# Experts of a small language-model tower: up products with the weights stationary, and the shared FFN by chunk

## What is computed

```python
h = take(W.T, x)                                   # 2048 rows of 128
h = h + mixer(layernorm(h))                        # tanh recurrence, gate, output product
xf = layernorm(h)                                  # [2048, 128]
idx, wts = top_1(xf @ gate_w.T)                    # one of 8 experts; softmax over one is 1
h1 = silu(xf @ w1[e].T) * (xf @ w3[e].T)           # inner width 512
y  = h1 @ w2[e].T                                  # back to 128
y += gelu(xf @ sw1.T) @ sw2.T                      # shared FFN, inner width 512
out = h + y
```

## Time and profile before

| | us |
|---|---|
| median of 3 runs | 190.79 (190.6 to 192.27) |
| the profiled execution | 191.11 |
| its span, first to last instruction | 189.3 |
| PE busy | 140.8 (74%) |
| DVE busy | 127.2 (67%) |
| ACT busy | 103.9 (55%) |
| POOL busy | 83.0 (44%) |

### The profile page before, as it was taken

How to read it: one execution, slowest core, us unless ns; L and a number is a source line. 1 busy time by engine, 2 the same in 40 slices (tenths; PEclk the granted TensorE clock), 3 DMA queues, 4 the chain that set the end, 5 groups by cost and what they waited for, 6 DMA issues and landing times.

```text
span 189.3 us, 3242 instructions
## 1 busy us (share of the span) xinstructions
PE 140.8 (74%) x1001; PEld 103.1 (54%) x1001; DVE 127.2 (67%) x364; ACT 103.9 (55%) x241; POOL 83.0 (44%) x77
## 2 busy tenths in 40 slices
PE   0106987697888888886894699990899999999710
PEld 0105865465666567763442699660476666776510
DVE  0245767838699857996681999651577888887720
ACT  2002343799569973787899970342256565666300
POOL 3767855500000001422000364373678888866580
PEclk9999999999999999999999579999589999999985
DMA  5663346994000000111100022321123243433331
GB/s 141 171 169 124 109 142 213 323 402 198 0 0 0 3 3 0 57 57 55 59 0 0 0 88 81 139 59 42 16 43 44 43 42 35 39 31 33 28 31 14
DMA packets 9955, 14.37 MB, mean 76 GB/s; under 512 B 1936, under 2 KB 4624, under 8 KB 9936
## 3 DMA queue, kind: packets, MB, share of 16 engines
q1 hardware_dynamic: 5904, 10.45, 16.1%
q0 software_dynamic: 4032, 3.67, 12.6%
HBM read 10.71 MB, written 3.41 MB: 75 GB/s over the span
## 4 chain that ended last, share of the span: by engine, by line
PE 40%; ACT 18%; DVE 11%; POOL 10%; issue 7%; DMA 7%; another core or an unknown queue 3%; SPq 1%; POOLq 0%
PE bank L647 13%; PE bank L592 7%; PE bank L674 7%; POOL emb_rows L364 6%; ACT attn_out L719 5%; PE bank L660 4%; ACT states L696 3%; DMA w_sb<-w 3%; DMA emb_rows<-emb,tok_sb 3%; PE bank L474 3%; ACT w_hl L729 3%; ACT states L755 2%; ACT w_hl L731 2%; POOL rstd L396 1%
## 5 line engine op out<-in xcount | busy, mean ns | idle before, releaser
L415 POOL DMA_INDIRECT out<-w_sb,row_of x20 | 31.4, 1570 | 13.7 <-DVE w_sb L1179 10.6
L474 PE MATMUL bank<-states,sq_sb 128*128 128x128 f32 x112 | 27.7, 331 | 6.4 <-ACT states L696 1.3
L647 PE MATMUL bank<-w_hl,xblk_t 128*128 x120 | 30.4, 392 | 0.6 <-issue 0.6
L474 PEld LDWEIGHTS bank<-states,sq_sb 128*128 128x128 f32 x112 | 17.8, 200 | 15.0 <-ACT states L696 14.2
L396 POOL TENSOR_TENSOR rstd<-vareps,cst 128x2 f32<-128x2 f32 x8 | 5.6, 697 | 46.6 <-DVE vareps L836 46.6
L472 PE MATMUL bank<-x_in,sq_sb 128*128 128x128 f32 x112 | 23.7, 295 | 2.2 <-ACT x_in L689 2.2
L797 ACT ACTIVATE w_sb<-bank,factor 128x512 f32<-128x512 f32 x20 | 13.8, 688 | 20.1 <-PE bank L647 14.6
L696 ACT ACTIVATE states<-bank 128x128 f32<-128x128 f32 x56 | 15.5, 276 | 14.9 <-PE bank L474 12.6
L674 PE MATMUL bank<-w_hl,w_sb 128*128 x160 | 17.5, 255 | 7.3 <-DVE w_sb L1179 7.3
L472 PEld LDWEIGHTS bank<-x_in,sq_sb 128*128 128x128 f32 x112 | 18.2, 203 | 3.4 <-ACT x_in L689 2.3
L408 POOL DMA_INDIRECT w_sb<-x_rows,row_in x16 | 15.4, 963 | 9.0 <-issue 6.9
(11 more groups left out here) (157 smaller groups left out, 284.2 us busy)
## 6 DMA issues: line engine op xcount, KB each, us to landing
w_sb<-w SPq DMA_DIRECT2D x24, 256.0 KB, 6.6
x_rows<-norm SPq DMA_DIRECT2D x4, 256.0 KB, 2.4
out<-attn_out SPq DMA_DIRECT2D x4, 256.0 KB
late<-places SPq DMA_DIRECT2D x1, 619.5 KB, 8.1
sw_sb<-sw SPq DMA_DIRECT2D x2, 256.0 KB
cst<-consts SPq DMA_DIRECT2D x1, 420.0 KB
sq_sb<-sq SPq DMA_DIRECT2D x1, 384.0 KB
out<-w_sb,row_of POOLq DMA_INDIRECT x20
```

The costliest lines, as they stand in the source:

```text
L415: pool.indirect_dma_start(out=out, out_offset=bass.IndirectOffsetOnAxis(ap=row_of[:, k:k + 1], axis=0), in_=out_blk[k % RING], in_offset=N ...
L474: pe.matmul(pre, at, states[:, i * COLS:(i + 1) * COLS], start=False, stop=True).then_inc(pre_ready, 1)
L647: mm = pe.matmul(hb[:], xblk_t[:, k % 3, b * P:(b + 1) * P], w[:, bass.ds(e * INNER + a * EXPERTS * INNER, INNER)], start=(j == 0), stop=( ...
```

## The change

- **Expert up products**: the weights become the stationary operand (128 columns of the inner width at a time), the transposed block the moving one. 24 matmuls of 128 columns in place of 6 of 512. The result has the inner width on its rows, so the transposes of the product and `turned` go; ACT and DVE take high and low half from `prod` in SBUF.
- **Two banks for the down product** (`ys`), and its wait for the output reaches back one block more.
- **Shared FFN by chunk**: `down_part(n)` runs the 12 matmuls of chunk n for four tiles as soon as `act_low` n is there; a product of zeros opens each group's bank. ACT takes high halves between the gelus, 8 behind (GELU_LEAD); gelu 0 comes inside the loop of pairs; the silu table is loaded behind the first `take_turned`. The inverse of the routing stands behind up product 13 (INVERT_AT = 14).
- **Gathers**: 16 ahead (AHEAD), each waiting for the landing of the one two before (IN_FLIGHT), a drain ahead of block 12.
- **Normalisation** of the last two pairs (LAST_NORMS) on DVE; **halves**: w1's upper high halves on ACT, all low halves of w2 before the attention end; SPREAD_STEPS 36 to 34, HIGH_STEP 38 to 36.

```diff
-SPREAD_STEPS = (22, 36)
-HIGH_STEP = 38
+SPREAD_STEPS = (22, 34)
+HIGH_STEP = 36
+GELU_LEAD = 8
+INVERT_AT = 14
+LAST_NORMS = 2
-AHEAD = 13
+AHEAD = 16
+IN_FLIGHT = 2
-DRAIN_AT = 6
-TURNED_FIRST = (1, 2, 2, 3, 4, 4, 5)
+DRAIN_AT = 12
-        rows_t, turned = (bank[3], bank[6]), (bank[4], bank[7])
+        rows_t, ys = (bank[3], bank[6]), (bank[6], bank[7])
...
             for k in range(AHEAD):
-                if 2 <= k < 5:
-                    pool.wait_ge(act_low, 4 * k)
-                elif k == 5:
-                    pool.wait_ge(base_ready, 3)
-                elif k >= 6:
-                    pool.wait_ge(blk_turned, TURNED_FIRST[k - 6])
                 if k == DRAIN_AT:
+                    pool.wait_ge(xblk_in[k - 1], 16)
                     pool.drain()
+                elif k >= IN_FLIGHT:
+                    pool.wait_ge(xblk_in[k - IN_FLIGHT], 16)
                 take_block(k)
...
+            def down_part(n):
+                g, i = divmod(n, IC)
+                if i == 0 and g >= 2:
+                    pe.wait_ge(base_ready, g - 1)
+                if i == 0:
+                    pe.matmul(bank[2 + g % 2][:], zeros[:], zeros[:, 0:1].to_broadcast([P, GC]), start=True, stop=False)
+                pe.wait_ge(act_low, n + 1)
+                for t in range(4):
                     for j, (a, b) in enumerate(halves):
                         mm = pe.matmul(bank[2 + g % 2][:, t * P:(t + 1) * P],
                                        (act_hi, act_lo)[a][:, g, i, t * P:(t + 1) * P],
                                        sw2_hl[:, b, i * P:(i + 1) * P],
-                                       start=(i == 0 and j == 0), stop=(i == IC - 1 and j == 2))
+                                       start=False, stop=(i == IC - 1 and t == 3 and j == 2))
...
-            for n in range(6, GROUPS * IC):
+            for n in range(6, INVERT_AT):
                 up(n)
+            pe.wait_ge(hots_ready, 1)
+            for t in range(TILES):
+                mm = pe.matmul(bank[4][:, 0:BLOCKS], lane_hot[:, :, t], nth_row[:, :, t],
+                               start=(t == 0), stop=(t == TILES - 1))
+            mm.then_inc(inverse_done, 1)
+            for n in range(INVERT_AT, GROUPS * IC):
+                up(n)
...
-            for m in range(TILES):
-                down(m)
-                if m == TILES - 4:
+            for n in range(GROUPS * IC):
+                down_part(n)
+                if n == GROUPS * IC - 3:
                     turn_block(0)
-                if m == TILES - 2:
-                    turn_block(1)
+            turn_block(1)
-            pe.wait_ge(w_split, 2)
+            pe.wait_ge(w_split, 3)
...
                     for w_hl, hb in ((w1_hl, bank[u]), (w3_hl, bank[2 + u])):
                         w = w_hl[:].rearrange("d h c -> d (h c)")
-                        for j, (a, b) in enumerate(halves):
-                            mm = pe.matmul(hb[:], xblk_t[:, k % 3, b * P:(b + 1) * P],
-                                           w[:, bass.ds(e * INNER + a * EXPERTS * INNER, INNER)],
-                                           start=(j == 0), stop=(j == 2))
+                        for i in range(IC):
+                            for j, (a, b) in enumerate(halves):
+                                mm = pe.matmul(hb[:, i * P:(i + 1) * P],
+                                               w[:, bass.ds(e * INNER + (a * EXPERTS * INNER + i * P), P)],
+                                               xblk_t[:, k % 3, b * P:(b + 1) * P],
+                                               start=(j == 0), stop=(j == 2))
                         mm.then_inc(h_done, 1)
...
-                if live(1):
-                    pe.wait_ge(prod_ready, k)
-                    if static is None or static >= 3:
-                        pe.wait_ge(prod_low, k - 2)
-                    for i in range(IC):
-                        mm = pe.transpose(turned[1 - u][:, i * P:(i + 1) * P], prod[:, 1 - u, i * P:(i + 1) * P], ident)
-                    mm.then_inc(prod_turned, 1)
                 if live(2):
                     pe.wait_ge(prod_low, k - 1)
-                    if static is None or static >= 3:
-                        pe.wait_ge(outb_ready, k - 2)
+                    if static is None or static >= 4:
+                        pe.wait_ge(outb_ready, k - 3)
...
-                            mm = pe.matmul(bank[6][:, 0:width], (prod_hi, prod_lo)[a][:, u, i * P:(i + 1) * P],
+                            mm = pe.matmul(ys[u][:, 0:width], (prod_hi, prod_lo)[a][:, u, i * P:(i + 1) * P],
...
-            act.wait_ge(w_split, 1)
-            for n in range(GROUPS * IC):
-                gelu(n)
-            act.activation(table_probe[:], half_bg[0:1, 0:1], ACT.Silu)
-            for n in range(GROUPS * IC):
-                act_high_half(n)
+            for n in range(1, GROUPS * IC + GELU_LEAD):
+                if n < GROUPS * IC:
+                    gelu(n)
+                if n >= GELU_LEAD:
+                    act_high_half(n - GELU_LEAD)
...
-                    act.wait_ge(prod_turned, k)
+                    act.wait_ge(prod_ready, k)
-                    act.activation(prod_hi[:, 1 - u, :], turned[1 - u][:], ACT.Copy).then_inc(prod_high, 1)
+                    act.activation(prod_hi[:, 1 - u, :], prod[:, 1 - u, :], ACT.Copy).then_inc(prod_high, 1)
...
             take_turned(0)
+            act.activation(table_probe[:], half_bg[0:1, 0:1], ACT.Silu)
             take_turned(1)
...
-            w1_low(slice(4 * INNER, 8 * INNER)).then_inc(w_split, 1)
+            dve.wait_ge(w1_high, EXPERTS // 2)
+            w1_low(slice(3 * INNER, 8 * INNER)).then_inc(w_split, 1)
...
+            def norm_last(n):
+                dve.wait_ge(rstd2_ready, n + 1)
+                for t in range(2 * n, 2 * n + 2):
+                    dve.tensor_scalar(norm2[:, t, :], attn_out[:, t, :], meanvar2[:, t, 0:1], rstd2[:, t:t + 1],
+                                      ALU.subtract, ALU.mult).then_inc(last_norm, 1)
...
-                    dve.tensor_tensor(prod_lo[:, 1 - u, :], turned[1 - u][:], prod_hi[:, 1 - u, :], ALU.subtract
+                    dve.tensor_tensor(prod_lo[:, 1 - u, :], prod[:, 1 - u, :], prod_hi[:, 1 - u, :], ALU.subtract
```

More of the change, by code:

```diff
@@ L235, in build @@
         table_probe = sb("table_probe", [1, 1])
+        zeros = sb("zeros", [P, P], F16)
         lane_hot = w1_sb[:, 2 * INNER:2 * INNER + TILES * P // 2].bitcast(F16).rearrange("q (p t) -> q p t", t=TILES)
@@ L560, in _ @@
                         pe.wait_ge(xffn_ready, n - 1)
-                    pe.wait_ge(norm2_ready, 2 * n + 2)
+                    if n < PAIRS - LAST_NORMS:
+                        pe.wait_ge(norm2_ready, 2 * n + 2)
+                    else:
+                        pe.wait_ge(last_norm, 2 * (n - PAIRS + LAST_NORMS) + 2)
                     for i in range(2):
@@ L766, in _ @@
                     act.activation(x_ffn[:, 0, n * PC:(n + 1) * PC], rows_t[n % 2][:, 0:PC], ACT.Copy).then_inc(xffn_high, 1)
+                if s == PAIRS:
+                    act.activation(table_probe[:], half_bg[0:1, 0:1], ACT.Gelu)
+                if s == PAIRS + 1:
+                    act.wait_ge(w_split, 1)
+                    gelu(0)
                 if 1 <= s and s + 1 < PAIRS:
                     gate(s + 1)
-                if s == PAIRS - 1:
-                    act.activation(table_probe[:], half_bg[0:1, 0:1], ACT.Gelu)
-                if 0 <= s - 2 < PAIRS:
+                if 0 <= s - 2 < PAIRS - LAST_NORMS:
                     n = s - 2
@@ L822, in _ @@
             dve.memset(piece[:, CHUNK - 1, :], 0.0).then_inc(seq_state, 1)
+            dve.memset(zeros[:], 0.0)
             dve.memset(x_at[:, :, :, 0:PADK], 0.0).then_inc(pads_zero, 1)
@@ L989, in _ @@
                 w3_low(j)
-            for j in range(EXPERTS - 5):
+            for j in range(EXPERTS - 3):
                 w2_low(j)
@@ L1104, in _ @@
                               ).then_inc(hots_ready, 1)
-            for n in range(4):
-                act_low_half(n)
+            act_low_half(0)
+            act_low_half(1)
             dve.wait_ge(inverse_done, 1)
             dve.tensor_scalar(row_in[:], bank[4][:, 0:BLOCKS], -1.0, 0.0, ALU.add, ALU.max).then_inc(index_ready, 1)
-            act_low_half(4)
-            act_low_half(5)
+            act_low_half(2)
+            act_low_half(3)
             then_wait(dve.scalar_tensor_tensor(out=spare[:], in0=bank[4][:, 0:BLOCKS], scalar=0.0,
@@ L1114, in _ @@
                                      op0=ALU.add, op1=ALU.add).then_inc(index_ready, 1)
-            act_low_half(6)
-            act_low_half(7)
+            for n in range(4, 8):
+                act_low_half(n)
+                if n == 6:
+                    take_down(0)
             k_e = lambda ap: ap.rearrange("q (k e) -> q k e", e=EXPERTS)
@@ L1160, in out_first @@
                     dve.wait_ge(y_done, k - 1)
[L1161 removed]
```

(3 more changed lines are left out.)

59 lines of the change are left out of this document (27 added, 32 removed).

## The result

The changed kernel takes 201.67 us (median of five executions, 198.45 to 205.12) against 190.79 us. The ratio to the kernel before is 1.043, 95% interval 1.034 to 1.052: slower. The medians count every execution, while the ratio compares fast executions with fast ones (198.45 to 199.83 us here) and so stands for 1.043 x 190.79 = 199.0 us. The forecast was 194.1 us, range 183 to 201.

The account below looks back on a forecast made before the run. PE was taken to bound the kernel. First up product at 115.6 us, 64.1 us of expert loop and a 12.9 us tail gave a 192.6 us span; plus 1.8, less 0.3, made 194.1 us, range 183 to 201.

Parts of the forecast that it names:

- Start of the expert loop: End of the shared FFN: first expert up product at 115.6 us instead of 120.17, 4.6 us earlier.
- the moved halves: Recurrence: moving half of w1's high half to ACT fills its spare time; at worst 0.2 us, taken as 0.
- Period set by PE's queue: Expert loop: PE's serial instruction queue, not its array (2.11 us), sets 3.34 us a block.
- 16 x 0.12 = 1.92 us: Expert up products: 16 register-computed weight addresses a block at 0.12 us each, beside 1.34 us of array work.
- blocks 2 to 18, 17 x 3.34 = 56.8: Expert loop: 17 blocks at 3.34 us take 56.8 us of the loop's 64.1 us.
- no gap over 3 us on PE from 97 to 180 us: Sign for the forecast: PE never stands over 3 us between 97 and 180 us.
- The hole: Early expert loop: PE's 5.23 us stall and its half clock, 7.7 us together, taken as gone without a gather burst.
- Rival 2: Early expert loop: PE's 5.2 us stall stays, from PE's own traffic, giving 200.9 us; chance 0.17.
- The gathers: POOL, two in flight: start near 101.3 us, come every 1.4 us, all 16 done at about 127 us.
- the ring: Four output blocks: DVE must wait for POOL's additions unless a block takes over 3 us.
- Tail: After the last up product: 12.9 us to the end of the span, unchanged.
- Rival 1: Expert loop: register work hidden, 2.17 us a block, POOL becomes the bound, 175.5 us; chance 0.17.

Follow-up runs that it names:

- e9: The changed kernel run again without an edit, for a second profile and more times: 201.47 us, ratio 1.050 to the kernel before.
- e3: Changed kernel's front and gathers with the expert loop of the kernel before (moving weights, product transposes, one down bank): 184.04 us, ratio 0.967.
- e6: Changed kernel with up and down addresses packed ahead of the waits, 20-block ending first, 12 gathers instead of 16 before the first addition: 181.84 us, ratio 0.957.
- e1: Changed kernel with the expert up products' weights at a fixed address, so no register instructions for their addresses: 184.9 us, ratio 0.971.
- e2: Changed kernel with a block's 16 weight addresses worked out together ahead of its up products, in 6 instructions: 191.89 us, ratio 1.004.
- e4: Changed kernel with PE running straight into the ending for 20 blocks, without the branch: 196.78 us, ratio 1.028.
- e5: Changed kernel with the branch kept and the ending for 20 blocks put first in the code: 198.48 us, ratio 1.033.
- e8: Kernel before with the changed kernel's expert loop alone; front, gathers and order of weight splits as before: 208.2 us, ratio 1.093.
- e11: e3 with 12 gathers instead of 16 ahead of the first addition (AHEAD = 12, DRAIN_AT = 10): 184.96 us, ratio 0.962.
- e10: The kernel before run again without an edit, for a second profile: 189.89 us (one execution).

## Why the prediction was right and wrong

The forecast of 194.1 us had the sign and the two main terms. It was 5 us under the 199.0 us of the ratio and 7.6 us under the median. Its sum against e9's profile:

- **Start of the expert loop: right.** 115.6 us forecast, 116.49 measured (115.2 and 115.6 in e3 and e6). The first gather was forecast at 101.3 us and began at 102.20. The half clock ahead of the loop went as expected. The 0.9 us are not lost in this stretch: from the first transpose of the attention end to the first up product e9 takes 39.43 us and e3 39.45, against 44.31 in the kernel before. They come from the recurrence, where the forecast took 0 for the moved halves and e9 has 3.4 us of half clock (attention end 1.2 us late). Whether the moved halves bring the half clock on is not shown.
- **Period set by PE's queue: right, its size a little small.** 3.34 forecast, 3.43 measured, and its main piece, "16 x 0.12 = 1.92 us", stands in the queue as forecast. e1 takes them away and the block falls to 2.1 to 2.3 us; e2 packs them and it falls to 2.6. Over 16 blocks the 0.09 us make 1.4 us. With 0.15 us for the first two blocks and 0.65 us for one block of 3.99 us, that is 2.2 us.
- **The missing term: the branch.** The step "blocks 2 to 18, 17 x 3.34 = 56.8" runs through block 18 as if nothing stood ahead of it. I had read the 0.28 us of issue at that place as a hiccup, and counted what the longer code costs while it runs, but not what it costs to jump over: 7.55 us to the next block instead of 3.43, 4.1 us. The forecast's own sign, no gap over 3 us on PE from 97 to 180 us, failed with it (3.95 us from 177.57 us). e4 and e5 take it away. Without it the forecast holds: e4 took 196.78 us, 1.4% above it.
- **The hole: its cost was right by luck, the reason fell.** "I take both as gone, since no burst of gathers is left". What is gone is most of its cost to PE: 0.6 us in e9 (counted above in the block of 3.99 us) and 1.2 us in the first profile. A wait of DVE is still there, 1.7 and 3.2 us behind PE's record. e8 has the burst and loses 1.3 us, e3 has no such wait at all, and e11, the same loop on the same front, has one again. What makes it was not found. Rival 2 (200.9 us) came out near the measured time by size and was still wrong: its 6.8 us are not in the trace, but 6.3 us of other causes are.
- **The gathers: 6 us late, at no cost here.** The forecast had all 16 done at about 127 us; in e9 the last is issued at 131.73 us and the first addition at 133.53. POOL stands 3.35 us at the drain, ahead of the gather of 126.42 us, which the forecast did not price. At 3.43 us a block this is hidden; e1 and e3, with shorter blocks, pay for it at the ring.
- **Tail: right.** 12.9 us forecast, 12.5 measured; last addition 6.4 us behind the last up product, as forecast.
- **Rival 1** (175.5 us, POOL the bound) has both halves shown: block time by e1, POOL's ring by e1 and e3. The change as it is never gets there, because DVE's outputs come slower (3.43 us) than POOL's pair (3.2 to 3.35 us).

The sum: 0.9 (start) + 2.2 (blocks) + 4.1 (branch) - 0.4 (tail) = 6.8 us over the forecast span of 192.6 us gives 199.4; the span was 199.3. By cause the 0.9 us of the start belong to the recurrence. The time of that execution lies 2.9 us over its span where I took 1.8.

## What to carry to other kernels

Where an operand's address hangs on a register, count the distinct addresses as instructions of the engine's queue, at the spacing of the queue (0.12 us here) and not at their own duration (32 and 46 ns), and set their sum beside the array's time before splitting a product into more and smaller ones; work them out together, and ahead of the waits, if they are many (e2 against e6: the same six instructions behind the waits still cost 0.3 us a block). When a program's unrolled code grows, look at every place where it branches over such code, and put the likely way first (here the place cost 4.1 us, and e5 took them away). A gain at the front is kept only if the loop behind it holds its pace: run the parts of a change apart, since here one part was worth 3.3% and the other cost more than all of it.

## What the hardware showed that was not expected

- A jump over 498 PE instructions cost 3.95 us of standing and one block at half clock behind it (24 pairs in 2.74 us, granted clock 0.50 from 181.5 to 184.3 us in e9); one over 312 cost 0.28 us. Jumps over 413 and 448 made the block 3.4 and 3.5 us longer.
- A register instruction with six operations works 74 ns where one with three works 46 ns and a lone addition 32 ns, but the next starts 0.13, 0.12 and 0.11 us after it. Its count, not its work, is what the queue pays: ten instructions less saved 0.8 us.
- Seven of the nine profiles with the front of after have TensorE's granted clock at half somewhere between 28 and 56 us, for 3.4 to 20.4 us; none of the four with the front of before has. The attention end then starts at 76.4 to 81.1 us instead of 75.1 to 75.9. In e9 PE had stood 1.88 us for ACT until 37.03 us, and the clock fell at 37.8. e3 and e6 have the same front and no fall, so this is not shown to be the change's doing.
- In the stall of before (both profiles), DVE and ACT wait for PE's counts while PE's own matmuls are recorded on schedule: the y product that e10 records at 125.35 to 126.17 us is taken up by DVE at 130.40. The same word stands for waits in the expert loops of all other profiles but e3, e4 and e5, at other places. The ends of matmuls are modelled in these profiles, so that the counts are late, and not the matmuls, is itself not certain. What holds them back stays open; no run isolates it.
